# Turning the inner values of an expert tile by DMA, and running its down products one up step later

## The reference

```python
x = x + tanh(g_xattn) * xattn(ctx, layernorm(x), Wq, Wk, gamma)      # (4, 512, 512)
x = x + tanh(g_ffn) * ffn(layernorm(x), ...)

def ffn(x, gate_w, gate_bias, shared_gw, shared_dw, up_w, down_w):
    xf = x.reshape(-1, 512)                                          # 2048 tokens
    y, g = split(xf @ shared_gw.T, 2)
    shared = silu(g) * y @ shared_dw.T
    scores = sigmoid(xf @ gate_w.T)
    _, topk_idx = top_k(scores + gate_bias, 2)                       # 2 of 8 experts
    w = take_along_axis(scores, topk_idx); w = w / sum(w)
    out = 0
    for e in range(8):
        we = sum(where(topk_idx == e, w, 0))
        g_e, u_e = split(xf @ up_w[e].T, 2)                          # 352 each
        out = out + (silu(g_e) * u_e) @ down_w[e].T * we
    return shared + out
```

## Time and profile before

| | |
|---|---|
| median of three runs | 544.96 us |
| the profiled execution, its own time | 546.4 us |
| its span, first to last instruction | 544.6 us |
| TensorE busy | 491.2 us (90%) |
| VectorE busy | 330.4 us (61%) |
| ScalarE busy | 255.4 us (47%) |
| GpSimd busy | 221.7 us (41%) |
| granted TensorE clock, mean | 0.959 of full |

### The profile page before, as it was taken

One profiled execution on the slowest core, in us unless ns is written; L12 is line 12 of the kernel. 1 busy time (PEld: TensorE's weight loads), 2 busy tenths in 40 slices (PEclk: granted clock), 3 DMA queues, 4 the chain that ended last, 5 costly groups with the idle time before them and its releaser, 6 DMA issues.

```text
span 544.6 us, 10400 instructions
## 1 busy us (share of the span) xinstructions
PE 491.2 (90%) x3021; PEld 271.8 (50%) x3022; DVE 330.4 (61%) x719; ACT 255.4 (47%) x465; POOL 221.7 (41%) x229
## 2 busy tenths in 40 slices
PE   7365998899979996899999999999999999999991
PEld 2233443444434444354655666665656665565650
DVE  1898799987888798779845774323333333323230
ACT  3683796776968496432312663222322222222220
POOL 2203268713984079401331444443334443344322
PEclk9669699999989998999999999999999999999997
DMA  6230332352443542140056897566565566656543
GB/s 212 113 103 21 120 101 70 97 177 89 132 112 99 187 108 77 72 166 2 0 149 233 231 259 132 98 110 112 101 111 97 106 102 113 112 97 108 98 55 39
DMA packets 45477, 61.57 MB, mean 113 GB/s; under 512 B 20544, under 2 KB 20800, under 8 KB 45440
## 3 DMA queue, kind: packets, MB, share of 16 engines
q1 hardware_dynamic: 36272, 40.53, 25.3%
q0 software_dynamic: 8736, 20.45, 21.7%
q10 hardware_dynamic: 432, 0.13, 0.1%
HBM read 37.90 MB, written 19.14 MB: 105 GB/s over the span
## 4 chain that ended last, share of the span: by engine, by line
PE 61%; DVE 20%; issue 5%; POOL 5%; ACT 5%; DMA 3%; DVEq 0%; POOLq 0%; ACTq 0%; SPq 0%
PE py L1121 14%; PE pg L1101 13%; PE pu L1102 12%; PE pg L949 5%; PE pu L949 5%; DVE w L1218 3%; DVE pa L1248 3%; PE pt_bank L883 3%; DVE w L1275 2%; PE pa L1111 2%; PE py L974 2%; DVE w L1252 2%; PE pa L1048 1%; DVE w L1198 1%; ACT w L666 1%
## 5 line engine op out<-in xcount | busy, mean ns | idle before, releaser
L1101 PE MATMUL pg<-w,x_t 128*128 x408 | 123.4, 313 | 0.3
L1102 PE MATMUL pu<-w,x_t 128*128 x408 | 123.3, 313 | 0.0
L569 POOL DMA_INDIRECT out<-rows,idx x39 | 61.8, 1585 | 136.7 <-ACT rows L816 125.7
L1121 PE MATMUL py<-w,work 128*128 x351 | 82.1, 379 | 0.8 <-DVE work L1606 0.8
L949 PE MATMUL pg<-w 128*128 128x512 f16 x288 | 77.3, 385 | 0.8 <-DVE work L1385 0.8
L806 ACT ACTIVATE work<-pg 128x352 f32<-128x352 f32 x39 | 18.1, 463 | 125.5 <-PE pu L1102 120.7
L949 PE MATMUL pu<-w 128*128 128x512 f16 x240 | 66.2, 385 | 0.0
L611 ACT ACTIVATE w<-stage 128x544 f16<-128x544 f32 x80 | 50.8, 648 | 31.5 <-DMA stage<-in_weights 31.0
L505 POOL TENSOR_TENSOR w<-stage,w 128x544 f16<-128x544 f32 x42 | 56.6, 1355 | 19.3 <-ACT stage L615 13.1
L1606 DVE COPY work<-pa 128x768 f16<-128x768 f16 x39 | 21.7, 557 | 62.3 <-PE pa L1111 57.9
L1595 DVE SCALAR_TENSOR_TENSOR work<-pu,work 128x352 f32<-128x352 f32 x39 | 20.5, 525 | 63.2 <-ACT work L806 59.6
(11 more groups left out here) (235 smaller groups left out, 810.3 us busy)
## 6 DMA issues: line engine op xcount, KB each, us to landing
stage<-in_weights SPq DMA_DIRECT2D x80, 272.0 KB
xn_rows<-w SPq DMA_DIRECT2D x16, 256.0 KB, 2.6
out<-w SPq DMA_DIRECT2D x16, 256.0 KB, 2.8
w<-in_x SPq DMA_DIRECT2D x3, 1024.0 KB, 5.5
w<-in_ctx_t SPq DMA_DIRECT2D x4, 256.0 KB, 4.0
w<-in_x SPq DMA_DIRECT2D x2, 512.0 KB, 3.8
out<-rows,idx POOLq DMA_INDIRECT x39, 5.0
work<-xn_rows,idx POOLq DMA_INDIRECT x20
```

Source lines behind the costliest of these rows:

```text
L569: pool.indirect_dma_start(out=out, out_offset=bass.IndirectOffsetOnAxis(ap=idx[:, t:t + 1], axis=0), in_=rows[:, t % 2, :], in_offset=None ...
L1101: pe.matmul(pg[p][:, 0:H], lhs, w[:, item, half, at:at + H], start=begin, stop=end)
L1102: mm = pe.matmul(pu[p][:, 0:H], lhs, w[:, item, half, at + H:at + 2 * H], start=begin, stop=end)
L1121: mm = pe.matmul(py[:, :], hid_t[:, p, part * JC + j, :], w[:, item, half, at:at + C], start=(j, part, half) == (0, 0, 0), stop=(j, part) ...
```

## The change

From tile 9 to tile 37 the inner values are turned by a DMA transpose from hid16 (128 x 768 values of two bytes) straight to hid_t, issued on SyncE (`turn_hidden`) ahead of the low-half transpose of tile t+3. Tiles 0 to 8 and the last keep the six TensorE turns. In the steps from tile 8 on TensorE's order becomes: turn of the rows of t+3, up(t+2), down(t) (`later_steps`); the last steps are up(38), down(36), down(37), inner turns of 38, down(38). The down products wait for the transpose (`ht_ld`), and the makers of hid16 for the transpose of two tiles before. ScalarE's output rows of t-2 now follow the inner values of t. GpSimd's program is not edited.

The diff, without the two constants and semaphores that it defines and without the mirrored lines of ScalarE and VectorE that only repeat the order:

```diff
@@ sync @@
+            def turn_hidden(t):
+                after(sp, hhi_sb, Q0 + t + 1)
+                after(sp, hlo_sb, Q0 + t + 1)
+                after(sp, down_mm, TILES + t - 1)
+                sp.dma_start_transpose(out=hid_t[:, t % 2, :, :], in_=hid16[:, t % 2, :, :].rearrange("p a c -> p (a c)")).then_inc(ht_ld[t % 2], 16)
+
+            for t in range(BY_DMA, TURN_FIRST + 3):
                 turn_low(t)
+            for t in range(TURN_FIRST, TURN_LAST + 1):
+                turn_hidden(t)
+                if t + 3 < SLOT_TILES:
+                    turn_low(t + 3)
@@ scalar @@
-            def hidden_high(t, p):
+            def hidden_high(t, p, turns=None):
                 after(act, hid_sb, Q0 + t + 1)
-                after(act, hid_mm, t - 1)
+                if turns is None:
+                    after(act, hid_mm, t - 1)
+                else:
+                    after(act, ht_ld[p], turns * 16)
                 act.activation(hid16[:, p, 0, 0:H], hid[:, p, :], ACT.Copy).then_inc(hhi_sb, 1)
...
+            for t in range(LATE_TILES, TURN_FIRST + 2):
+                silu(t, t % 2)
+                hidden_high(t, t % 2)
+                if t < TURN_FIRST:
+                    expert_rows(t - 1, (t - 1) % 2)
+                elif t > TURN_FIRST:
+                    expert_rows(t - 2, t % 2)
+            with act.Fori((TURN_FIRST + 1) // 2, SLOT_TILES // 2) as i:
                 for k in range(2):
                     t = i * 2 + k + 1
                     silu(t, 1 - k)
-                    hidden_high(t, 1 - k)
-                    expert_rows(t - 1, k)
+                    hidden_high(t, 1 - k, i - (TURN_FIRST - 1) // 2)
+                    expert_rows(t - 2, 1 - k)
+            expert_rows(SLOT_TILES - 2, 1)
@@ tensor @@
-            def down(t, p, item):
-                after(pe, ht_sb, t + 1)
+            def down(t, p, item, turns=None):
+                if turns is None:
+                    after(pe, ht_sb, t + 1)
+                else:
+                    after(pe, ht_ld[p], turns * 16)
                 after(pe, y_sb, TILES + t)
...
+            def later_steps(t0, n0, turned=0):
+                up_item = item_of(t0 + 2)
+                for k in range(GATHERS):
+                    turn_gathered(t0 + k + 3, (k + 3) % GATHERS, n0 + (k + 3) // GATHERS, blocks=KC)
+                    low, low_n = (k + 2) % GATHERS, n0 + (k + 2) // GATHERS - BY_DMA // GATHERS + 1
+                    up(t0 + k + 2, k % 2, ds(up_item, 1), range(KC), low, low_n)
+                    if k == 0:
+                        down_item, next_item = item_of(t0), item_of(t0 + 1)
+                    last_item, up_item = up_item, item_of(t0 + k + 3) if k < GATHERS - 1 else None
+                    down(t0 + k, k % 2, ds(down_item, 1), None if k < turned else n0 * 2 + turns_by_dma(k))
+                    down_item, next_item = next_item, last_item
+
             loops = (SLOT_TILES - 3) // GATHERS
             assert loops * GATHERS == SLOT_TILES - 3
             for i in range(2):
                 expert_steps(i * GATHERS, i, GATHERS, late=True, dma_from=BY_DMA - i * GATHERS)
-            with pe.Fori(2, loops) as i:
-                expert_steps(i * GATHERS, i, GATHERS)
+            later_steps(2 * GATHERS, 2, turned=TURN_FIRST - 2 * GATHERS)
+            with pe.Fori(3, loops) as i:
+                later_steps(i * GATHERS, i)
             t = SLOT_TILES - 3
-            expert_steps(t, t // GATHERS, 1, turn=False)
-            t = SLOT_TILES - 2
-            down(t, t % 2, ds(item_of(t), 1))
-            turn_hidden(t + 1, (t + 1) % 2)
-            down(t + 1, (t + 1) % 2, ds(item_of(t + 1), 1))
+            low_n = t // GATHERS - BY_DMA // GATHERS + 1
+            up(t + 2, 0, ds(item_of(t + 2), 1), range(KC), (t + 2) % GATHERS, low_n)
+            down(t, 0, ds(item_of(t), 1), turns_by_dma(t))
+            down(t + 1, 1, ds(item_of(t + 1), 1), turns_by_dma(t + 1))
+            turn_hidden(t + 2, 0)
+            after(pe, ht_sb, TURN_FIRST + 1)
+            down(t + 2, 0, ds(item_of(t + 2), 1), 0)
@@ vector @@
-            def hidden_low(t, p):
+            def hidden_low(t, p, turns=None):
                 after(dve, hhi_sb, Q0 + t + 1)
-                after(dve, hid_mm, t - 1)
+                if turns is None:
+                    after(dve, hid_mm, t - 1)
+                else:
+                    after(dve, ht_ld[p], turns * 16)
                 dve.tensor_tensor(hid16[:, p, 1, 0:H], hid[:, p, :], hid16[:, p, 0, 0:H], ALU.subtract).then_inc(hlo_sb, 1)
...
-            with dve.Fori(LATE_TILES // 2, (SLOT_TILES - 3) // 2) as i:
+            for t in range(LATE_TILES, TURN_FIRST + 2):
+                hidden(t, t % 2)
+                hidden_low(t, t % 2)
+                gathered_turned(t + 2, t % 2, t + 1, blocks=KC)
+                if t < TURN_FIRST:
+                    hidden_turned(t, t % 2)
+            with dve.Fori((TURN_FIRST + 1) // 2, (SLOT_TILES - 3) // 2) as i:
                 for k in range(2):
-                    hidden_rows(i * 2 + k + 1, 1 - k)
+                    t = i * 2 + k + 1
+                    hidden(t, 1 - k)
+                    hidden_low(t, 1 - k, i - (TURN_FIRST - 1) // 2)
+                    gathered_turned(t + 2, 1 - k, t + 1, blocks=KC)
```

More of the change, by code:

```diff
@@ L41 @@
 BY_DMA = 8
+TURN_FIRST, TURN_LAST = 9, 37
 SMALL = 2
@@ L261, in build @@
         g_ld = [sem(f"g_ld{n}") for n in range(GATHERS)]
+        ht_ld = [sem("ht_ld0"), sem("ht_ld1")]
         xl_ld = [sem(f"xl_ld{n}") for n in range(GATHERS)]
@@ L294, in late_pieces, with turns_by_dma @@
             return [(LATE + k // CHUNKS, k % CHUNKS) for k in range(begin, min(begin + PER_TILE, (ITEMS - LATE) * CHUNKS))]
+        def turns_by_dma(t):
+            return (t - TURN_FIRST) // 2 + 1
         def scaled_pieces(item, n):
@@ L427, in turn_low @@
                 sp.dma_start_transpose(out=x_low[t % GATHERS], in_=xg_slots[t % GATHERS][:, C:2 * C]).then_inc(xl_ld[t % GATHERS], 16)
-            for t in range(BY_DMA, SLOT_TILES):
+            def turn_hidden(t):
[4 more added lines that the diff above has]
+            for t in range(BY_DMA, TURN_FIRST + 3):
                 turn_low(t)
+            for t in range(TURN_FIRST, TURN_LAST + 1):
+                turn_hidden(t)
+                if t + 3 < SLOT_TILES:
+                    turn_low(t + 3)
             after(sp, rows_free, SLOT_TILES)
@@ L829, in _ @@
                     high_piece(*piece)
-            with act.Fori(LATE_TILES // 2, SLOT_TILES // 2) as i:
+            for t in range(LATE_TILES, TURN_FIRST + 2):
[6 more added lines that the diff above has]
+            with act.Fori((TURN_FIRST + 1) // 2, SLOT_TILES // 2) as i:
                 for k in range(2):
@@ L1108, in turn_hidden @@
                 after(pe, hlo_sb, Q0 + t + 1)
-                after(pe, ht_sb, t - 1)
+                after(pe, ht_sb, min(t - 1, TURN_FIRST))
                 for n in range(2 * JC):
@@ L1596, in hidden @@
                                          in1=hid[:, p, :], op0=ALU.mult, op1=ALU.mult).then_inc(hid_sb, 1)
-            def hidden_low(t, p):
+            def hidden_low(t, p, turns=None):
                 after(dve, hhi_sb, Q0 + t + 1)
-                after(dve, hid_mm, t - 1)
+                if turns is None:
+                    after(dve, hid_mm, t - 1)
+                else:
+                    after(dve, ht_ld[p], turns * 16)
                 dve.tensor_tensor(hid16[:, p, 1, 0:H], hid[:, p, :], hid16[:, p, 0, 0:H], ALU.subtract).then_inc(hlo_sb, 1)
             def hidden_turned(t, p):
-                after(dve, hid_mm, t + 1)
+                after(dve, hid_mm, min(t, TURN_FIRST) + 1)
                 after(dve, down_mm, TILES + t - 1)
@@ L1619, in _ @@
             shared_rows(BATCHES - 1, TPB - 1)
[L1621 to L1626, removed]
             for t in range(LATE_TILES):
@@ L1636, in _ @@
                     low_piece(*piece)
-            with dve.Fori(LATE_TILES // 2, (SLOT_TILES - 3) // 2) as i:
+            for t in range(LATE_TILES, TURN_FIRST + 2):
[5 more added lines that the diff above has]
+            with dve.Fori((TURN_FIRST + 1) // 2, (SLOT_TILES - 3) // 2) as i:
                 for k in range(2):
-                    hidden_rows(i * 2 + k + 1, 1 - k)
+                    t = i * 2 + k + 1
+                    hidden(t, 1 - k)
+                    hidden_low(t, 1 - k, i - (TURN_FIRST - 1) // 2)
+                    gathered_turned(t + 2, 1 - k, t + 1, blocks=KC)
             for t in range(SLOT_TILES - 2, SLOT_TILES):
-                hidden_rows(t, t % 2, turned=False)
+                hidden(t, t % 2)
+                hidden_low(t, t % 2, turns_by_dma(t - 2))
+            hidden_turned(SLOT_TILES - 1, 0)
 def kernel(x, ctx_512, g_xattn, g_ffn, L0_xattn_Wq, L0_xattn_Wk, L0_xattn_gamma_raw, L0_ffn_gate_w, L0_ffn_gate_bias,
```

## The result

The changed kernel takes 585.11 us in the median of four runs (582.04 to 587.78), the kernel before 545.54 beside it; the ratio is 1.072 (95% interval 1.066 to 1.079), slower. The forecast was slower, 575 us with a range of 563 to 593; the time lies inside it, 10 us above the 575. The profiled execution has a span of 586.0 us against 544.6; its own time, 587.78 us, is the longest of the four. Five executions of e5_dma, e7_before_loads and e8_order_gather_loads ran at a mean granted clock of 0.56 to 0.83, where 0.95 is usual, and took 593 to 857 us; the ratios leave them out.

What follows compares the result with a forecast made beforehand. TensorE, 90% busy, bounded the kernel before; after the change, a two-tile loop through the gather, 14.5 us, would. Tile stretch +31.2 and tail -0.8 made +30.4 us: 575 us on the median, range 563 to 593.

Steps and rivals of the forecast that it cites:

- the gather becomes the wait: TensorE's row turns of n+3, now right behind down(n-1): the gather lands at 8.45 us, needed at 5.74; wait 2.7 or more.
- The links: Two-tile loop: down to scatter 1.86, to gather 1.89, landing 4.7, start-up 0.1, turns, up and down 5.74; 14.3 us.
- the wide transpose is covered: SyncE's inner-value transpose, about 3 us in all, lands before the down products, 11.5 us later even without any wait.
- the 13 that would bind: Rival, wide transpose on SyncE binds the down products if it takes over 13 us; 599 us at 16; chance 0.03.
- The share of the DMA engines: Wide transpose's packets share engines with scatter and gather: 0.2 us per two-tile loop, bounds 0 and 1.0.
- The tail: From the end of down(35) to the end: scatters set the end, 25.3 us against 26.1, so -0.8.
- The three loads: Three tile-number loads before the first down of each loop of four: 1.4 us in all, bounds 0 and 2.8.
- The first two tiles: D(7) to D(9) on TensorE: 9.88 us to D(8), gather not late there, then 5.74 to D(9).
- Rival B: Clock falls in TensorE's gaps, idle 3.0 us in each of 13 loops of 14.5 us; chance 0.11.
- a clock at 0.5 after the gaps: Sign against the forecast, which expected granted clock near 1.0 in the tile stretch.
- The sum: D(7) to D(35): 205.5 us against 174.3, +31.2; with the tail's -0.8, total +30.4 us.
- Rival A: Gather in time on TensorE, under 5.74 us after D(n-2): period 5.86, 538 us, not slower; chance 0.04.

Runs made afterwards that it cites:

- e5_dma: Changed kernel with TensorE's and ScalarE's old order and the loads where they were, tiles 9 to 37 still turned by DMA: 546.72 us, ratio 1.002.
- e7_before_loads: Kernel before with only the second tile-number load of each loop of four moved into the middle of the up products: 542.99 us, ratio 0.9945.
- e8_order_gather_loads: As e3_both (moved order, earlier gathers, spread loads), but inner values turned by TensorE, without wide DMA transposes: 547.80 us, ratio 1.003.
- e4_order: Kernel before with the moved TensorE order from tile 8 and ScalarE's output rows moved, no wide DMA transpose: 582.63 us, ratio 1.074.
- e2_gather: Changed kernel with each gather issued one step earlier on GpSimd, gather(t+5) before scatter(t): 550.57 us, ratio 1.008 to the kernel before.
- e9_before_both: Kernel before with the second tile-number load moved into the up products and the gathers one step earlier: 544.43 us, ratio 0.998.
- e1_loads: Changed kernel with only the three tile-number loads spread out (inside up, behind up, behind down): 580.68 us, ratio 1.069 to the kernel before.
- e3_both: Changed kernel with the gathers one step earlier and the three tile-number loads spread out: 547.55 us, ratio 1.010 to the kernel before.
- e5_again: Single later run of the same kernel as e5_dma (DMA turns with the old order): 546.92 us.

## Why the prediction was right, point by point

The mechanism was forecast and is shown. That the total missed by 10 us only is in part luck: terms that were too small or left out came to some 17 us, and a loop estimated too long gave 5 us back.

*That the gather becomes the wait, and why: right, and shown.* The links were forecast as 1.86, 1.89, 4.7, 0.1 and 5.74 us, the contention as 0.2; the loop above has 1.83, 1.89, 4.39 and 5.98. It is 14.09 against 14.5, and the wait in it is 2.2 us, not 3.0; the mean of all thirteen loops, 15.2, holds the loads and the clock below as well. e4_order shows that the moved order suffices for the loss, e2_gather that an earlier gather removes it.

*That the wide transpose is covered: right.* There was no wait of the down products for it; its landing, 4.4 us in the median and 6.9 at most, is far from the 13 that would bind. Only its size was off: 1.24 us of engine time, not 1.0.

*The share of the DMA engines, 0.2 us per loop: no more than that shows.* The scatter's landing, as in the earlier trace rows, is 5.0 us in the median as before, and only its maximum has grown:

```profile
DMA to landing us min/median/max: 4.6/5.0/7.6
```

Of the upper bound, 1.0 us per loop, this median shows nothing. The 7.6 us are the scatter of 348.28, just before the first wide transpose (350.81); but e9_before_both, which has no wide transpose, has a landing of 7.4, so the cause of such single ones stays open.

*The tail, -0.8: right,* it was -0.7.

*The three loads, 1.4 us in all: mis-sized, and outside my bounds of 0 to 2.8.* They cost 10.2 us of waits on six of the seven loop turns from tile 8 on. I took the loop's turn of before, one load ahead of a down and two behind it, as the measure; three in a row are 1.5 to 1.9 us each time. With them moved apart (e1_loads) the time falls by 4.4 us in the runs.

*The first two tiles, 15.6 us: short by 3.4.* Down(7) to down(8) took 12.2, not 9.9, of which 1.85 are the first three loads. Another 0.8 us was the wait for the gather of tile 12, which landed 7.2 us after its issue (350.17 to 357.34), beside the first wide transpose; no row read before the change had one so late.

*Rival B, the clock: a third of it came true.* The forecast had the full clock through all 13 loops, and a clock at 0.5 after the gaps was named as a sign of being wrong; the earlier trace rows have a gap with such a fall behind it and one without. There were four stretches of 3.4 us at a granted clock of 0.50 among the tiles, about 1.7 us each, 7 us. Around two gaps, columns as in the earlier trace rows:

```profile
438.05:440.52 2.47, 0.00 (x0) 0.00 (x1) 0.52 (x1) 0.69 (x1) 0.52 (x1) 1.00 0.44 128
441.84:445.25 3.41, 3.41 (x14) 1.77 (x12) 0.00 (x0) 0.00 (x0) 0.98 (x1) 0.50 1.05 150
468.40:470.40 2.00, 0.00 (x0) 0.00 (x0) 0.49 (x1) 0.69 (x1) 0.30 (x1) 1.00 0.46 132
471.00:474.00 3.00, 3.00 (x21) 2.04 (x22) 0.33 (x1) 0.00 (x0) 1.68 (x2) 1.00 0.78 90
```

The gap of 2.47 us was followed by a stretch at 0.50, the second one was not. The length of the gap doesn't decide it: of the ten gaps of 1.98 to 2.47 us four were followed by such a stretch at 0.50, among them the shortest, 1.98 us before 547.26, and one of 2.19 us (before 456.31, then 1.00) was not. The granted clock over the tile stretch is 0.97, where it was 1.00.

*The sum.* +31.2 us were forecast for the tile stretch, +42.2 measured. The loads, those of tile 8 among them, account for +8.8 of the 11 (a part of which replaces waiting for the gather), the clock for up to 7, the late gather of tile 12 for 0.8, and the shorter loop gives back 13 x 0.4 = 5. These are estimates from single waits and stretches, and add up to 11.6.

*Rival A, 538 us if the gather were in time: wrong in its price.* e3_both is that case, made by an edit, and takes 547.55. The period was taken as 5.86, TensorE's own, and the scatter chain was put below it at 5.58, a figure of the tail; beside gathers and transposes the scatters of e3_both stand 6.2 us apart. Had the gather been in time, the change would still have brought nothing.

## What to carry to other kernels

When work is moved on one engine, follow the buffers of every other engine whose program isn't touched: here the row turns came one down earlier while the gather that feeds them stayed behind the scatter of a fixed tile, and 8.1 us had to fit where 5.7 were left. Before taking work off the busiest engine, find the next floor with all of its neighbours running: the chain of scatters stood at about 6.2 us per tile beside TensorE's 6.2, and none of the kernels that took 0.34 us per tile off TensorE without running late on the gather (e2_gather, e3_both, e5_dma) was faster than the one before. And where a loop's turn with two register loads behind a down and one ahead of it costs 0.46 us, three in a row can cost 1.5 to 1.9.

## What the runs showed of the hardware

In the changed kernel TensorE's loads of a register from tile_e took 0.30 us at least, 0.39 in the median and 1.15 at most (60 of them), and three in a row held the down products back by 1.5 to 1.9 us. A wide DMA transpose (128x768, two-byte values) issued there in 1.21 us in the median (1.84 at most), hardly longer than the narrow one (128x512, 1.19), where I had assumed 1.8, and landed in 4.4 us there and in 3.1 in e5_again (medians). After the changed kernel's gaps of 2.0 to 2.5 us the granted clock fell to 0.50 for 3.4 us in four cases and stayed at 1.00 in six; which gaps it follows these runs do not settle.
